# Half-row tiles for siblings, three banks a ring in attention, and column copies one tap ahead, in a four-layer pre-norm kernel

## The reference

```
x = x + L0(gn(x))   # 1x1 conv, group norm, silu, a pooled gate network, learned basis functions, 1x1 conv
x = x + L1(gn(x))   # in-projection, 3x3 depthwise conv, silu; KV = B^T V; y = C KV + xs D; y*silu(z); layer norm; out-projection
x = x + L2(gn(x))   # attention: 8 heads of 8 channels over 256 positions
x = x + L3(gn(x))   # deformable 3x3 conv: offsets and mask from a conv, bilinear samples, weight per tap
```

```
scores = einsum('bhqd,bhkd->bhqk', q, k) * scale
attn = softmax(scores, axis=-1)
ctx = einsum('bhqk,bhkd->bhqd', attn, v)
```

## Time and profile before

| | |
|---|---|
| median of 3 runs | 598.48 us |
| profiled execution, its own time | 598.75 us |
| its span | 597.0 us |
| mean granted TensorE clock | 0.872 |
| TensorE busy | 439.6 us (74%) |
| VectorE busy | 379.7 us (64%) |
| ScalarE busy | 278.7 us (47%) |
| GpSimd busy | 93.2 us (16%) |

### The profile page before, as it was taken

How to read it: one execution, slowest core, us unless ns; L and a number is a source line. 1 busy time by engine, 2 the same in 40 slices (tenths; PEclk the granted TensorE clock), 3 DMA queues, 4 the chain that set the end, 5 groups by cost and what they waited for, 6 DMA issues and landing times. The chain is left out here.

```text
span 597.0 us, 9930 instructions
## 1 busy us (share of the span) xinstructions
PE 439.6 (74%) x3042; PEld 230.1 (39%) x3042; DVE 379.7 (64%) x724; ACT 278.7 (47%) x471; POOL 93.2 (16%) x79
## 2 busy tenths in 40 slices
PE   2317641999999536556899999965448998989995
PEld 1116531545544214113455555423324444444441
DVE  4347776123356779645688999732256878878874
ACT  0469952041342215024466666641546557475331
POOL 6700004000000007000000000010004508154000
PEclk9757985899999869558799999986857999999999
DMA  5300002500000004553210000007655090642302
GB/s 140 82 0 1 0 0 66 110 0 1 0 0 0 0 1 111 153 160 107 72 38 3 1 1 1 1 1 165 159 114 126 16 221 2 155 82 56 64 2 70
DMA packets 22557, 34.05 MB, mean 57 GB/s; under 512 B 5361, under 2 KB 17793, under 8 KB 21761
## 3 DMA queue, kind: packets, MB, share of 16 engines
q1 hardware_dynamic: 20224, 31.12, 21.4%
q10 hardware_dynamic: 2304, 2.58, 2.1%
HBM read 16.68 MB, written 4.64 MB: 36 GB/s over the span
## 5 line engine op out<-in xcount | busy, mean ns | idle before, releaser
L944 ACT ACTIVATE L_e<-L_ring 128x512 f32<-128x512 f32 x128 | 71.9, 596 | 67.0 <-PE L_ring L989 66.4
L867 DVE TENSOR_REDUCE L_mx<-L_ring 128x2 f32<-128x512 f32 x128 | 82.7, 683 | 29.3 <-PE L_ring L978 27.8
L1235 DVE TENSOR_TENSOR L_s<-L_row_ps,L_cols 128x1024 f32<-128x1024 f32 x72 | 88.0, 1223 | 19.0 <-ACT L_cols L1292 16.6
L1372 PE MATMUL L_acc<-L_s,L_t_sb 128*64 128x256 f32 x576 | 79.8, 399 | 14.7 <-DVE L_s L1235 14.0
L1292 ACT ACTIVATE L_cols<-L_col_ps 128x512 f32<-128x512 f32 x72 | 42.9, 596 | 63.4 <-PE L_col_ps L1361 40.5
L978 PE MATMUL L_ring<-stacks_k_st,stacks_q_st 128*128 (+1 forms) x256 | 54.9, 301 | 12.2 <-DMA stacks_k_st<-L_k_parts 8.3
L989 PE MATMUL L_ring<-stacks_q_st,stacks_k_st 128*128 (+1 forms) x128 | 50.2, 397 | 15.6 <-DMA stacks_q_st<-L_m_parts 15.4
L1372 PEld LDWEIGHTS L_acc<-L_s,L_t_sb 128*64 128x64 f32 x576 | 35.6, 138 | 50.4 <-DVE L_s L1235 30.9
L1358 PE MATMUL L_row_ps<-L_hats,L_sel 48*128 48x512 bf16 x144 | 44.6, 392 | 0.2 <-DVEq L1226 0.2
L633 PE MATMUL L_xs_ps<-L_stack,L_w_tap 128*128 (+1 forms) x96 | 44.1, 600 | 0.0
L978 PEld LDWEIGHTS L_ring<-stacks_k_st,stacks_q_st 128*128 (+1 forms) x256 | 21.5, 101 | 44.9 <-issue 26.9
(11 more groups left out here) (249 smaller groups left out, 734.2 us busy)
## 6 DMA issues: line engine op xcount, KB each, us to landing
L_hats<-L_parts SPq DMA_DIRECT2D x32, 216.0 KB, 4.7
L_hat<-L_offsets SPq DMA_DIRECT2D x24, 192.0 KB, 4.6
stacks_q_st<-L_q_parts SPq DMA_DIRECT2D x48, 64.0 KB
stacks_k_st<-L_k_parts SPq DMA_DIRECT2D x24, 128.0 KB
L_mask<-L_offsets SPq DMA_DIRECT2D x12, 192.0 KB, 4.7
L_q_parts<-L_parts SPq DMA_DIRECT2D x8, 192.0 KB, 2.9
L_k_parts<-L_parts SPq DMA_DIRECT2D x8, 192.0 KB, 3.1
L_stack<-L_xpad SPq DMA_DIRECT2D x8, 162.0 KB, 5.6
```

Of the source, the lines that this page charges most:

```text
L867: dve.tensor_reduce(mx[:, b, :, head], ring[:, k % 2].rearrange("p (q s) -> p q s", q=2), AX.X, ALU.max).then_inc(max_read, 1)
L944: act.activation(e[:, k], ring[:, 2 + k % 2], ACT.Exp, scale=HD2 ** -0.5).then_inc(e_ready, 1)
L1235: dve.tensor_tensor(s[:, q], row_ps[:, q], cols[:, q:q + 1].broadcast_to([P, 2, 2 * N]), ALU.mult).then_inc(s_ready, 1)
L1372: mm = pe.matmul(acc[C * e:C * e + C, b, 0:N], t_sb[:, b, h, (KK * e + t) * C:(KK * e + t + 1) * C], s[:, q, h, e * N:(e + 1) * N], start= ...
```

## The change

**Layer 1.** The load of `conv_w` now brings the third filter row to both halves, so its upper half is not zero, and the fill of zeros goes. In `conv_xs`, groups 0 to 2 stay. For the third filter row, each half of the array now does other images: two sibling matmuls of 64 rows and 256 columns, h = 0 in partitions 0 to 63 (images 2h + e) and h = 1 in 64 to 127, with the shift undone in the address. `proj_z` is split in the same way. `conv_bc` takes 64 rows for groups 3 to 5. TensorE's loop over quads is written out, with the pieces of the convolution cut at 2, 4, 8, 12 instead of 3, 5, 9, 12.

**Layer 2.** `q_st` has one copy of 128 partitions. `largest` uses the 64 partitions of its head's half. `scores` is now two matmuls of 64 rows and 256 columns, for one head instead of two. In a row of the new order the maxima's step is 17 ahead of the scores' (`LAG`), so the two use different halves. The ring has six banks, three for each use; the context has one bank for two, and the maxima share the other small bank. Stack loads are 12 a group, six of them in ScalarE's queue for the first two groups. The context matmuls come in half lumps. ScalarE takes the copy of the turned context and the negation of the maxima, and GpSimd their split into two parts, from VectorE. All loops but SP's last are written out.

**Layer 3.** `spread` is cut in two: the columns of tap v + 2 are spread when the rows of tap v + 1 are, and copied into one of three buffers. The normalize goes to ScalarE, the addition moves to after tap 1 of the next pair, `WEIGHED` is (2, 3, 4, 5, 6, 7), the hat steps are twelve, as absolute value and relu are two steps, and loops are written out.

The diff, cut to its core:

```diff
-WEIGHED = (1, 2, 3, 5, 6, 7)
+WEIGHED = (2, 3, 4, 5, 6, 7)
...
+        self.loads[1] += [(cw[C * e:C * e + C, 3 * k:3 * k + 3, :], ins["conv_w"][min(2 * k + e, 2):min(2 * k + e, 2) + 1].broadcast_to([C, 3, DI + 32]))
+                          for k, e in ((0, 0), (0, 1), (1, 0), (1, 1))]
...
-                        h, g = divmod(k, 6)
-                        mm = pe.matmul(xs_ps[:, 2 * h:2 * h + 2, :], w_tap[:, g, 0:DI], tap(stack, 4 * q + 2 * h, g, 2),
-                                       start=(g == 0), stop=(g == 5))
+                        if k < 6:
+                            h, g = divmod(k, 3)
+                            pe.matmul(xs_ps[:, 2 * h:2 * h + 2, :], w_tap[:, g, 0:DI], tap(stack, 4 * q + 2 * h, g, 2),
+                                      start=(g == 0), stop=False)
+                        else:
+                            g, e = 3 + (k - 6) // 2, k % 2
+                            for h in range(2):
+                                rows = slice(C * h, C * h + C)
+                                taps = image(stack[rows], 4 * q + 2 * h + e)[:, :, 2 - h:2 - h + H, g - 3:g - 3 + W]
+                                mm = pe.matmul(xs_ps[:, 2 * h + e:2 * h + e + 1, :], w_tap[rows, g, 0:DI], taps, start=False, stop=(k == 11))
                     if stop == 12:
...
                 def proj_z(q):
                     for h in range(2):
-                        mm = pe.matmul(z_ps[:, 2 * h:2 * h + 2, :], w_z[:], image(stack, 4 * q + 2 * h, 2)[:, :, 1:1 + H, 1:1 + W],
+                        rows = slice(C * h, C * h + C)
+                        mm = pe.matmul(z_ps[:, 2 * h:2 * h + 2, :], w_z[rows], image(stack[rows], 4 * q + 2 * h, 2)[:, :, 1 - h:1 - h + H, 1:1 + W],
                                        start=True, stop=True)
...
-    LOADS = 12 + 6
+    LOADS = 6 + 6
+    LAG = 17
+    ROWS = range(-LAG, 8 * (B + 2))
...
+        ring, ctx_ps, a_ps = m.ps("ring", [P, 6, 2 * N]), m.ps("ctx_ps", [P, 2 * N]), m.ps("a_ps", [P, 2 * N])
+        m_ps = a_ps[0:8, N:2 * N]
+        k_bank = lambda g: [ring[:, 4], ring[:, 5], ctx_ps[:], a_ps[:]][g]
...
+        def load_stacks(eng, g, s):
+            eng.wait_ge(stacks.filled, 2 * g + 2)
+            eng.wait_ge(stored[2 * g + s], 32)
+            for slot, part in enumerate(((0, 0, 0, 1, 1, 2), (0, 1, 2, 0, 1, 0))[s]):
+                src = scratch[s][g, part].rearrange("e d p b n -> (e d) (p b n)")
+                dst = (q_st, k_st)[s][slot:P:SLOTS, g]
+                eng.dma_start(dst.rearrange("r p b n s -> r (p b n s)"), src).then_inc(stacked[g], 16)
...
+                load_stacks(sp, 0, 0)
                 store_parts(1)
-                load_stacks(1, 0)
-                load_stacks(1, 1)
+                load_stacks(sp, 1, 0)
+                send_maxima(0, 0)
                 store_parts(2)
-                send_maxima(0, 0)
+                send_maxima(0, 1)
+                load_stacks(sp, 2, 0)
+                send_maxima(0, 2)
+                load_stacks(sp, 2, 1)
                 store_parts(3)
-                send_maxima(0, 1)
-                load_stacks(2, 0)
-                load_stacks(2, 1)
-                send_maxima(0, 2)
-                load_stacks(3, 0)
                 send_maxima(0, 3)
-                load_stacks(3, 1)
+                load_stacks(sp, 3, 0)
+                load_stacks(sp, 3, 1)
                 with sp.Fori(1, NQ) as i:
                     for j in range(4):
                         send_maxima(i, j)
@@ -829,12 +833,17 @@
...
+                    pool.wait_ge(m_read, n + 1)
+                    pool.wait_ge(m_stacked, 64 * n + 64)
+                    pool.tensor_copy(m_parts[:, b, 0], m_neg[:, b]).then_inc(m_hi, 1)
+                    pool.wait_ge(m_hi, n + 1)
+                    pool.tensor_tensor(m_parts[:, b, 1], m_neg[:, b], m_parts[:, b, 0], ALU.subtract).then_inc(m_ready, 1)
...
+                def exponents(v):
+                    c, k = divmod(v, 8)
+                    act.wait_ge(s_ready, v + 1)
+                    if k % 4 == 0 and c:
+                        act.wait_ge(ev_done, 2 * c - 1 + k // 4)
+                    act.activation(e[:, k], ring[:, 3 + v % 3], ACT.Exp, scale=HD2 ** -0.5).then_inc(e_ready, 1)
+                def take_maxima(n):
+                    act.wait_ge(mx_turned, n + 1)
+                    if n > 1:
+                        act.wait_ge(m_ready, n - 1)
+                    act.activation(m_neg[:, n % 2], m_ps, ACT.Copy, scale=-1.0).then_inc(m_read, 1)
+                def take_turned(c):
+                    act.wait_ge(ctx_back, c + 1)
+                    if c:
+                        act.wait_ge(o_ready, c)
+                    act.activation(ctx_c[:], a_ps[:, 0:P], ACT.Copy).then_inc(ctx_copied, 1)
+                def take_context(c):
+                    act.wait_ge(ev_done, 2 * c + 2)
+                    if c > 1:
+                        act.wait_ge(ctx_turned, c - 1)
+                    act.activation(ctx[:, c % 2].rearrange("p g n -> p (g n)"), ctx_ps[:], ACT.Copy).then_inc(ctx_ready, 1)
+                for v in ROWS:
+                    c, k = divmod(v, 8)
+                    if 0 <= v < 8 * B:
+                        exponents(v)
+                    if k == 0 and image_of(c + 1):
+                        take_maxima(c + 1)
+                    if k == 1 and image_of(c - 2):
+                        take_turned(c - 2)
+                    if k == 2 and image_of(c - 1):
+                        take_context(c - 1)
...
+                def rows_of(st, n, h, p):
+                    g, j = divmod(n, 4)
+                    return st[C * h:C * h + C, g, p, j % 2, j // 2, :]
...
+                def largest(step):
+                    n, k = divmod(step, 8)
                     h, p = k % 2, k // 2
-                    g, j = at
-                    pe.wait_ge(max_read, 8 * n + k + 1)
+                    if step % 32 == 0:
+                        pe.wait_ge(stacked[step // 32], LOADS * 16)
+                    if step > 2:
+                        pe.wait_ge(max_read, step - 2)
                     for q in range(2):
-                        mm = pe.matmul(ring[:, k % 2, q * N:(q + 1) * N], q_st[:, h, ds(g, 1), p, j % 2, j // 2, q * P:(q + 1) * P], k_st[:, ds(g, 1), p, j % 2, j // 2, :],
+                        mm = pe.matmul(ring[:, step % 3, q * N:(q + 1) * N], rows_of(q_st, n, h, p)[:, q * P:(q + 1) * P], rows_of(k_st, n, h, p),
...
+                def scores(v):
+                    c, k = divmod(v, 8)
+                    h, p = k % 2, k // 2
                     if k == 0:
                         pe.wait_ge(m_stacked, 64 * c + 192)
-                    pe.wait_ge(e_ready, 8 * c + k + 1)
-                    pe.matmul(ring[:, 2 + k % 2], k_st[:, ds(g, 1), p, j % 2, j // 2, t * P:(t + 1) * P], q_st[:, :, ds(g, 1), p, j % 2, j // 2, :],
-                              start=True, stop=True).then_inc(s_ready, 1)
-
-                def context(c, b, g):
-
-                    pe.wait_ge(e_ready, 8 * c + 4 * g + 6)
-                    pe.wait_ge(v_x_ready, c + 1)
...
+                def turn_maxima(n):
+                    pe.wait_ge(max_read, 8 * n + 8)
+                    if n > 2:
+                        pe.wait_ge(ctx_normed, 2 * (n - 3) + 2)
+                    elif n:
+                        pe.wait_ge(m_read, n)
...
+                for v in ROWS:
+                    c, k = divmod(v, 8)
+                    if v + LAG < 8 * B:
+                        largest(v + LAG)
+                    if 0 <= v < 8 * B:
+                        scores(v)
+                    if k == 0 and image_of(c - 2):
+                        turn_back(c - 2)
+                    if k == 0 and image_of(c + 1):
+                        turn_maxima(c + 1)
+                    if k in (1, 2) and image_of(c - 1):
+                        context(c - 1, 1, k - 1)
+                    if k == 3 and image_of(c - 2):
+                        project(c - 2)
+                    if k == 5 and image_of(c - 1):
+                        turn_context(c - 1)
+                    if k in (6, 7) and image_of(c):
+                        context(c, 0, k - 6)
 
 
...
-        cols, s = m.sb("cols", [P, 2, 2 * N]), m.sb("s", [P, 2, 2, 2 * N])
+        cols, s = m.sb("cols", [P, 3, 2 * N]), m.sb("s", [P, 2, 2, 2 * N])
...
+                def norm(n):
+                    act.wait_ge(col_ready, 15 * n - 23)
+                    act.activation(xn[:, n % 2, :], x[:, n, :], ACT.Identity, scale=gn.scale[:, n:n + 1], bias=gn.shift[:, n:n + 1]).then_inc(xn_ready, 1)
+                hat_steps = ((take_distance, 0), (make_hat, 0), (take_distance, 1), (make_hat, 1), (take_first, 0), (take_distance, 2),
+                             (make_hat, 2), (take_first, 1), (take_second, 0), (take_first, 2), (take_second, 1), (take_second, 2))
+                for hat_step, j in hat_steps:
                     hat_step(0, j)
                 for k in range(6):
```

(27 more changed lines are left out.)

369 lines of the change are left out of this document (146 added, 223 removed).

## The result

The changed kernel takes 588.65 us, median of four runs (584.11 to 592.46), against 598.66 (598.20 to 599.05): ratio 0.9835, 95% interval 0.9805 to 0.9865. It is faster by 10 us, not by 33, and lies outside the predicted range. Its runs lie 8 us apart, those of before 1 us. The profiled execution took 588.86, with a span of 587.1 and a mean granted clock of 0.840 (before 0.872).

What follows compares the result with a forecast made beforehand. It took layer 1 as bound by TensorE, layer 2 by TensorE and VectorE waiting for each other, layer 3 by a chain near TensorE's pace. 598.75 - 10.5 - 13.5 - 9.5 = 565.3 us, range 547 to 580.

Steps and rivals of the forecast that it cites:

- Layer 1: Convolution and gate projection: paired 64-row matmuls at half cost save 10.5 us, bounds -13 and -5.
- Layer 2, start: Layer 2's opening: stack loads shared by two queues and earlier maxima sends, 12.9 us gained up to image 4.
- Layer 2, steady: Layer 2's loop: 7.75 us an image against 7.79, a gain of 0.4 us over 11 images.
- The ring: Layer 2's loop: waits from first scores through context, GpSimd's v_x and split, and sends to next scores; 7.3 to 8.3 us.
- the bound of 8.3: Layer 2's loop: longest image length allowed, in us, with which layer 2 gains only 7.
- Layer 2, tail: Layer 2 after the last scores: nearly the same chain as before, no gain or loss put on it.
- Layer 3: Column copy a tap ahead and normalize on ScalarE gain 15 us, less 6 for stalls: -9.5, bounds -2 and -16.
- three stalls: Layer 3: hats come late for the next image's first column spread, about 2 us three times, 6 us lost.
- A: Layers 1 and 2: 64-row tiles gain nothing or lose it to changes of tile size; 582 us, chance 0.1.
- price for a change of tile size: TensorE, layers 1 and 2: 0.13 us per change, 8 more an image in layer 2 being 1.0 us.
- B: Layer 2's loop: the ring is shorter than read, an image takes 6.9 us; 556 us, chance 0.18.
- The rival of the other side: Layer 2's ring at 10.8 us an image or more, through slow GpSimd, eats all gain; 612 at 12; chance 0.04.

Runs made afterwards that it cites:

- e8: The kernel before with only layer 1 and its weights' load from the change: 587.44 us, ratio 0.9813.
- e7: e3 with the loads of stacks 2 and 3 sent four at a time after each image's maxima sends in layer 2: 540.67 us, ratio 0.9034.
- e4: Changed kernel with 10 filler products of 128 rows ahead of each image's wait for its maxima in layer 2: 573.70 us, ratio 0.9583.
- e10: e7 with LAG 16 instead of 17, so a row's maxima and scores use the same half of the array: 571.37 us, ratio 0.9484.
- e3: Changed kernel with GpSimd splitting the maxima before it copies v_x in layer 2: 558.73 us, ratio 0.9317.
- e12: Changed kernel with two 64-row filler products ahead of each scores row from the middle of image 14 on: 585.66 us, ratio 0.9704.
- e5: Changed kernel with 10 filler products of 64 rows ahead of each image's wait for its maxima in layer 2: 573.56 us, ratio 0.9546.

## Why the prediction was wrong, step by step

The sum was 565.3; the profiled execution took 588.86. Of the 23.6 us, layer 1 is 3.4, layer 2 is 21.6, layer 3 is -0.6 and layer 0, which differs by up to 1.8 between kernels that share its code, -0.8.

**Layer 1** (-10.5 predicted, -7.1 in the changed kernel, -10.2 in e8). The mechanism was right, the size a little too large: six siblings of the convolution and the six full products take 8.2 us (119.14 to 127.36) where 7.8 was forecast and 10.57 is the earlier trace rows; loop quads, transposes to transposes, take

```profile
148.77 1.07 PE L666 MATMUL L_t_ps<-all_ident,L_xs 128*128 128x128 f32 x8 [0.59 <-ACT L_xs L603]
...
166.07 1.07 PE L666 MATMUL L_t_ps<-all_ident,L_xs 128*128 128x128 f32 x8 [0.59 <-ACT L_xs L603]
```

17.30 us where 16.9 was forecast and 19.55 is the earlier trace rows; the wait for the activation of the earlier trace rows stands where it was put, 0.59. Three loop quads gave 6.7 instead of 8.1, the part ahead of them 1.9 instead of 2.4: 8.7 of the 10.5. The rest is the last quad's clock, which the sum took as unchanged: it cost 1.6 us here and gave 1.1 in e8.

**Layer 2, start** (-12.9 up to image 4): right to 0.1 us. In the time of before, the scores of image 0 were set at 253.3 and those of image 4 at 291.2; layer 2 now starts 7.90 us earlier (207.34 against 215.24), which makes 245.4 and 283.3, and the trace has 245.36 and 283.20. In between it was less exact: the first step came 1.0 us late, and images 2 and 3 started their scores at 259.78 and 270.21, 1.1 and 1.2 us ahead of what was set. SyncE's queue, walked in order, is a sound instrument to about 1 us; that the ends meet within 0.1 is luck. The image 4 of before stands at 304.37, not at 304.1. What the prediction didn't say is that this was a loss to be had back: e7.

**Layer 2, steady** (7.75 an image): the step that failed. The ring was read rightly: GpSimd's order of v_x and split, the place at row 0 where TensorE waits, VectorE idle behind it. Its length at full clock is 8.20 at best, not 7.75: the first part, to the copy of v_x, 2.76 (356.58 to 359.34) instead of 2.5, GpSimd 1.37 as forecast (1.35), sends and landing 4.1 instead of 3.8. Over images 4 to 15 e4, at full clock, has 8.30 an image: 0.55 x 11 = 6.0 us, at the bound of 8.3. The term that was missing is the clock. The prediction had TensorE busy 6.9 of 7.75 us, idle for 0.85 in every image, and kept all its durations at 2.4 GHz. The clock fell behind those waits in five of the ten images from 283.20 to 372.99, which stretched TensorE's part of the ring by 1.1 us (3.78 against 2.66) in the image shown. From image 4 to image 15 the changed kernel takes 99.4 us, e4 91.3: 8.1. In the earlier trace rows TensorE was busy 73.6 of 75 us in layer 2, so its 1.00 was no promise; the earlier trace rows held the hint, four matmuls in 1.01 us at 243.67 behind a wait of 8.34.

**Layer 2, tail** ("nearly the same chain"): the same instructions, but from the first scores of image 15 at 382.55 to the next layer's normalization at 401.10 it took 18.55 us; e4, at full clock, took 12.9. About 5.6 us, the clock again. All in all the clock explains 14 of the 21.6 (what e4 gave back), the ring's length 6. The last 2 are the tail at full clock: with its images taken as in the loop, the sum leaves 11 us from image 15's scores to the end, and e4 has 12.9.

**Layer 3** (-9.5 predicted, -10.1 measured): the mechanism was right, the closeness partly luck. Additions of images 0, 1 and 2 of the changed kernel:

```profile
469.25 0.47 DVE L1262 SCALAR_TENSOR_TENSOR all_x<-L_acc,all_l_vec,all_x 128x256 f32<-128x256 f32 x1
...
486.66 0.47 DVE L1262 SCALAR_TENSOR_TENSOR all_x<-L_acc,all_l_vec,all_x 128x256 f32<-128x256 f32 x1
...
502.67 0.47 DVE L1262 SCALAR_TENSOR_TENSOR all_x<-L_acc,all_l_vec,all_x 128x256 f32<-128x256 f32 x1
```

An image without hats to wait for takes 16.01 (15.9 forecast), the other 17.41, so the wait is 1.4 where 2 was taken, once in two images as said. The 17.8 of the earlier trace rows is an average of two lengths as well: before, the additions of images 0 to 3 stand at 469.69, 486.51, 505.79 and 522.61, so 16.8 and 19.3 in turn. From image 0's addition to image 5's the kernel went from 88.97 to 84.02, 4.9 us, where 9.4 less 6 for three stalls, 3.4, was forecast; the rest of the layer gave 5.1 where 5.7 was put. The terms as written add up to 9.1 and not 9.5, and layer 2's to 13.3 and not 13.5, which changes nothing.

**Rivals.** A fell: siblings start 0.01 us apart, and e10 shows 1.18 us an image lost without them. Its price for a change of tile size was too high: in the changed kernel a row of siblings between two context lumps takes 340.70 - 340.37 = 0.33 us, of which 0.21 are columns, so 0.12 for both changes and not 0.13 each. TensorE's own image is 6.65 (e7), not 6.9. The Trainium skill, TensorEngine Tiling (Array Packing), Tiling Modes, says that a change of mode drains TensorE; this row agrees that something is paid, half of what the prediction took. B did not happen in the changed kernel. e3 makes its case by another program, an image at TensorE's pace, and took 558.7 against the 556 given for it. The rival of the other side had the right place, the same ring, and a wrong idea of what would lengthen it: GpSimd was on time, TensorE was slow.

What stays open: what brings the clock back once it has fallen (e10 to e12), why it falls behind one wait and not behind another as long, and why some executions lose it and others of the same kernel don't.

## What to carry to other kernels

Where a change makes TensorE wait once in every round of a loop, price that loop at 1.2 GHz as well; here an image in which the clock fell took 9.57 us on the average and one in which it stayed 8.38, and the tail, entered behind such a wait, lost 5.6 us. An engine with spare time is not a free place for a step on the critical ring: look at what its program puts ahead of the step (GpSimd, 8% busy, held the maxima until a context product two images older was done, and swapping two of its statements gave 30 us). The same goes for a DMA queue: bulk loads belong behind the small urgent sends, in pieces that fit between them (13.5 us of layer 2).

## What the runs showed that was not expected

- The granted clock fell in a loop whose waits were all under 2 us (1.27 at 329.33, 1.84 at 319.67), with TensorE busy 3.99 of the 5 us before. Five of the ten images from 283.20 on had a fall, with waits ahead of them of 1.26, 1.27, 1.31, 1.84 and, in the opening, 3.70 us; the five without had 0.60, 0.69, 0.94, 1.16 and 1.27. The two of 1.27 show that the wait alone doesn't decide it.
- It can stay low for long with TensorE without a gap: 25.00 of 25 us busy at 0.50 in e10, 19.80 of 20 in the changed kernel's tail; while in e3 and e7 the same tail stayed at 1.00 (busy 13.3 of 14 us in e3 and 12.4 of 13 in e7).
- Filler products made a kernel 15 us faster (e4, e5), and 64 rows did as well as 128 there.
- The runs of one kernel spread over 1 to 4 us before (4 to 13 runs in a set), 8 us in the changed kernel and in e3, 3 us in e7 and 25 us in e10 (four runs each).
